# Row-maximum parts moved from VectorE to GpSimd in a two-batch attention and mixture kernel

## The reference

```python
scores = jnp.einsum('bhqd,bhkd->bhqk', Q, K) / jnp.sqrt(jnp.float32(D_HEAD))
scores = jnp.where(causal, scores, jnp.float32(-jnp.inf))
A = jax.nn.softmax(scores, axis=-1)
AV = jnp.einsum('bhqk,bhkd->bhqd', A, V)
```

## Time and profile before

| What | Value |
|---|---|
| Median of 2 runs | 432.5 us (432.46 to 432.53) |
| The profiled execution, its own time | 433.2 us |
| Its span | 431.3 us |
| PE busy | 406.8 us (94%) |
| VectorE busy | 307.0 us (71%) |
| ScalarE busy | 243.2 us (56%) |
| GpSimd busy | 78.4 us (18%), 115 instructions |
| Granted TensorE clock, mean | 0.996 |

### The profile page before, as it was taken

How to read it: one execution, slowest core, us unless ns; L and a number is a source line. 1 busy time by engine, 2 the same in 40 slices (tenths; PEclk the granted TensorE clock), 3 DMA queues, 4 the chain that set the end, 5 groups by cost and what they waited for, 6 DMA issues and landing times.

```text
span 431.3 us, 7424 instructions
## 1 busy us (share of the span) xinstructions
PE 406.8 (94%) x2570; PEld 214.3 (50%) x2570; DVE 307.0 (71%) x807; ACT 243.2 (56%) x541; POOL 78.4 (18%) x115
## 2 busy tenths in 40 slices
PE   7998899999999989999999999999999998999994
PEld 3545444353333544566768844335334344446783
DVE  5538997798799666528478799789879863213765
ACT  5691564766777666543441265667666847642421
POOL 4331210243151010102230021113312011020000
PEclk9999999999999999999999999999999999999998
DMA  6066761450403000001764046054130000000011
GB/s 196 10 101 98 191 105 18 62 88 3 76 2 98 1 2 0 2 1 46 134 124 66 8 91 93 10 86 67 17 60 3 0 3 1 2 0 2 0 50 49
DMA packets 18452, 21.14 MB, mean 49 GB/s; under 512 B 4976, under 2 KB 11888, under 8 KB 18416
## 3 DMA queue, kind: packets, MB, share of 16 engines
q1 hardware_dynamic: 18365, 20.66, 25.7%
q10 hardware_dynamic: 51, 0.01, 0.0%
HBM read 5.79 MB, written 2.10 MB: 18 GB/s over the span
## 4 chain that ended last, share of the span: by engine, by line
PE 74%; DVE 16%; ACT 6%; issue 2%; DMA 1%; POOL 1%; ACTq 0%; DVEq 0%; POOLq 0%
PE ps L951 17%; PE ps L1066 14%; PE ps L1045 14%; PE ps L1022 10%; DVE mx L822 9%; PE ps L959 8%; PE ps L967 4%; PE ps L942 2%; PE ps L1026 2%; ACT pr L681 2%; PE ps L1140 1%; PE ps L1076 1%; DVE ps L818 1%; ACT stk L602 1%; ACT qk_raw L667 1%
## 5 line engine op out<-in xcount | busy, mean ns | idle before, releaser
L681 ACT ACTIVATE pr<-ps 128x512 f32<-128x512 f32 (+3 forms) x384 | 165.9, 495 | 95.2 <-PE ps L1045 93.7
L822 DVE TENSOR_REDUCE mx<-ps 128x1 f32<-128x512 f32 (+3 forms) x240 | 145.6, 666 | 14.5 <-PE ps L1022 7.4
L1045 PE MATMUL ps<-stq,stk 99*128 99x512 bf16 (+3 forms) x384 | 116.2, 330 | 4.4 <-ACT pr L681 3.3
L1022 PE MATMUL ps<-stk,stq 96*128 96x512 bf16 (+3 forms) x384 | 112.7, 327 | 1.9 <-DVE mx L822 0.9
L593 POOL TENSOR_SCALAR_AFFINE_SELECT pr<-pr 128x512 f32<-128x512 f32 x64 | 40.9, 639 | 248.0 <-ACT pr L681 248.0
L1066 PE MATMUL ps<-pr,va 128*32 128x512 f32 (+3 forms) x768 | 81.8, 498 | 0.0
L1045 PEld LDWEIGHTS ps<-stq,stk 99*128 99x128 bf16 x384 | 34.4, 98 | 90.4 <-ACT pr L681 52.0
L1022 PEld LDWEIGHTS ps<-stk,stq 96*128 96x128 bf16 x384 | 37.5, 98 | 22.4 <-issue 6.8
L818 DVE CUSTOM_DVE_ANT_0 ps<-ps,causal 128x384 f32<-128x384 f32 (+1 forms) x64 | 38.6, 648 | 11.6 <-PE ps L1022 11.6
L1026 PE MATMUL ps<-mask,ident_b 128*128 128x128 bf16 x192 | 35.4, 219 | 0.0
L951 PE MATMUL ps<-u_t,avt 128*128 128x256 f32 x128 | 30.8, 384 | 0.3 <-ACT avt L717 0.2
(11 more groups left out here) (108 smaller groups left out, 391.0 us busy)
## 6 DMA issues: line engine op xcount, KB each, us to landing
stq<-qk_raw SPq DMA_DIRECT2D x32, 96.0 KB, 2.8
stk<-qk_raw SPq DMA_DIRECT2D x32, 96.0 KB, 2.8
x_in<-in_x SPq DMA_DIRECT2D x8, 256.0 KB, 3.7
stq<-qk_raw SPq DMA_DIRECT2D x32, 64.0 KB, 2.4
stk<-qk_raw SPq DMA_DIRECT2D x32, 64.0 KB, 2.4
out_y<-x SPq DMA_DIRECT2D x3, 512.0 KB, 3.4
stk<-qk_raw SPq DMA_DIRECT2D x32, 32.0 KB, 2.4
stq<-qk_raw SPq DMA_DIRECT2D x32, 32.0 KB, 2.1
```

Source lines behind the costliest of these rows:

```text
L681: nc.scalar.activation(probs(b, g, s)[:, j, q0 - c * CHUNK:], act_bank(ev)[:, q0 - c * CHUNK:], ACT.Exp, scale=DH ** -0.5).then_inc(s_act_ ...
L822: nc.vector.tensor_reduce(dst, src, AX.X, ALU.max).then_inc(s_dve_free, 1)
L1022: last = nc.tensor.matmul(bank[:, i * w:(i + 1) * w], q[0:ROWS, t // TPC, j, tile(t % TPC)], k[0:ROWS, k0 // CHUNK, j, 0:w], start=True, s ...
L1045: nc.tensor.matmul(bank[:, q0 - c * CHUNK:], stk[stack_of(b, g)][0:ROWS + PARTS, kt // TPC, j, tile(kt % TPC)], stq[stack_of(b, g)][0:ROWS ...
```

## The change

The four instructions of every `split` go to GpSimd. VectorE keeps the reductions and, for the second chunk, the maximum over both halves, which now raises a semaphore of its own, `s_joined`. GpSimd handles `split` at its place in the list and waits for the last maximum (first chunk) or for `s_joined` (second chunk), and for the `rows` matmul that read the parts of the block before it. Each of its four instructions waits for the one before through `s_residue`; the last raises `s_split`, for which PE waits as before.

```diff
+                if kind == "split":
+                    _, _, g, c = ev
+                    whole, n = mx[:, g % 2, c, 0], 3 * (n_split[ev] - 1)
+                    pool.wait_ge(*((s_joined, n_joined[ev]) if c else (s_dve_free, n_last[ev])))
+                    if b * G + g:
+
+                        pool.wait_ge(s_act_full, n_act["rows", *divmod(b * G + g - 1, G), c])
+                    pool.tensor_copy(mhl[:, c, 0], whole).then_inc(s_residue, 1)
+                    pool.wait_ge(s_residue, n + 1)
+                    pool.tensor_tensor(mres[:], whole, mhl[:, c, 0], ALU.subtract).then_inc(s_residue, 1)
+                    pool.wait_ge(s_residue, n + 2)
+                    pool.tensor_copy(mhl[:, c, 1], mres[:]).then_inc(s_residue, 1)
+                    pool.wait_ge(s_residue, n + 3)
+                    pool.tensor_tensor(mhl[:, c, 2], mres[:], mhl[:, c, 1], ALU.subtract).then_inc(s_split, 1)
...
                 if kind == "split":
                     _, _, g, c = ev
 
-                    dve.wait_ge(s_dve_free, last_max)
-                    whole = mx[:, g % 2, c, 0]
                     if c:
-
-                        link(nc.vector.tensor_tensor(whole, mx[:, g % 2, c, 0], mx[:, g % 2, c, 1], ALU.max))
-                    if b * G + g:
-
-                        dve.wait_ge(s_act_full, n_act["rows", *divmod(b * G + g - 1, G), c])
-                    link(nc.vector.tensor_copy(mhl[:, c, 0], whole))
-                    link(nc.vector.tensor_tensor(mres[:], whole, mhl[:, c, 0], ALU.subtract))
-                    link(nc.vector.tensor_copy(mhl[:, c, 1], mres[:]))
-                    nc.vector.tensor_tensor(mhl[:, c, 2], mres[:], mhl[:, c, 1], ALU.subtract).then_inc(s_split, 1)
+                        dve.wait_ge(s_dve_free, n_last[ev])
+                        nc.vector.tensor_tensor(mx[:, g % 2, c, 0], mx[:, g % 2, c, 0], mx[:, g % 2, c, 1], ALU.max).then_inc(s_joined, 1)
```

More of the change, by code:

```diff
@@ L370, in block_kernel @@
         s_split = sem("s_split")
+        s_joined = sem("s_joined")
+        s_residue = sem("s_residue")
         s_rows = [sem(f"s_rows{i}") for i in range(2)]
@@ L406, in block_kernel @@
         n_logits = count("lg")
+        n_last, n_joined = {}, {}
+        for ev in order:
+            if ev[0] == "max":
+                latest = n_dve[ev]
+            if ev[0] == "split":
+                n_last[ev] = latest
+                n_joined[ev] = len([e for e in n_last if e[3]])
         n_split, n_rows = count("split"), count("rows")
@@ L822, in _ @@
                         nc.vector.tensor_reduce(dst, src, AX.X, ALU.max).then_inc(s_dve_free, 1)
-                    last_max = n_dve[ev]
                 if kind == "split":
                     _, _, g, c = ev
-                    dve.wait_ge(s_dve_free, last_max)
-                    whole = mx[:, g % 2, c, 0]
                     if c:
-                        link(nc.vector.tensor_tensor(whole, mx[:, g % 2, c, 0], mx[:, g % 2, c, 1], ALU.max))
-                    if b * G + g:
-                        dve.wait_ge(s_act_full, n_act["rows", *divmod(b * G + g - 1, G), c])
-                    link(nc.vector.tensor_copy(mhl[:, c, 0], whole))
-                    link(nc.vector.tensor_tensor(mres[:], whole, mhl[:, c, 0], ALU.subtract))
-                    link(nc.vector.tensor_copy(mhl[:, c, 1], mres[:]))
-                    nc.vector.tensor_tensor(mhl[:, c, 2], mres[:], mhl[:, c, 1], ALU.subtract).then_inc(s_split, 1)
+                        dve.wait_ge(s_dve_free, n_last[ev])
+                        nc.vector.tensor_tensor(mx[:, g % 2, c, 0], mx[:, g % 2, c, 0], mx[:, g % 2, c, 1], ALU.max).then_inc(s_joined, 1)
                 if kind == "turn":
```

## The result

The changed kernel took 463.9 us (463.63 to 464.15, two runs) against 432.5: a ratio of 1.072, with a 95% interval of 1.070 to 1.074. The forecast was 459, its range 449 to 470. The profiled execution took 463.6 us with a span of 461.8.

A forecast was written before the change was run, and what follows sets the result against it. PE was taken to bound the kernel, holding 74% of the chain. Late masks and parts add 21.8 us and clock falls 4.8, together 26.6 on the 432.5 us median: 459 us predicted, range 449 to 470.

The forecast's parts named there:

- What stands behind the split: On GpSimd, masks PE needs earlier stand behind a split that now waits for VectorE, so they come late.
- The sum of the waits: New PE waits over both batches: 11.6 us in batch 0 and 10.2 in batch 1, together 21.8 us.
- the price of a split on GpSimd: From last maximum to finished parts on GpSimd: four instructions of 0.18 or 0.21 and 0.14 hand-overs, 1.34 us.
- The Trainium skill's factor of two: Two-input elementwise work about twice as slow on GpSimd as VectorE: subtraction 0.34 us, 2.9 us more over eleven places.
- Block (1,1) as the longest: At (1,1) `value` waits for a mask behind the split and two `bo` additions: 4.79 us late in batch 0.
- The clock: PE's clock falls to half in the two longest of four long waits only: 2 x 2.4 = 4.8 us.
- The price per fall: Each clock fall costs 2.4 us, estimated from twenty PE fillers after an idle engine, 7.00 us against 4.58.
- The rival with four falls: Masks late and the clock falls in all four long waits, adding 9.7 us: 464 us, chance 0.22.
- What VectorE gains is hidden: VectorE's busy time falls by some 11 us without use, as it has caught up with PE after such waits.
- Only the latency counts: Rival: VectorE runs close enough behind PE for timely masks; eleven places cost 0.50 us each: 438 us, chance 0.06.

The follow-up runs named there:

- the masks ahead: Changed kernel, with GpSimd taking one or two masks, and the `bo` or `far` between, ahead of the split at five blocks: 434.4 us, ratio 1.0044.
- (1,1) alone: Kernel before, VectorE still splitting, with GpSimd only waiting for the split at block (1,1) in both batches: 443.5 us, ratio 1.026.
- (0,1) alone: Kernel before, VectorE still splitting, with GpSimd only waiting for the split at block (0,1) in both batches: 442.8 us, ratio 1.023.
- seven splits moved: Kernel before, with seven of sixteen splits on GpSimd where PE had not waited, masks ahead at (1,1) and (3,1): 432.6 us, ratio 0.9995.
- `bo` and `far` behind the mask: Changed kernel, with GpSimd's `bo` additions at (1,1) and `far` at (2,1) put behind the first mask: 457.3 us, ratio 1.056.
- fillers inside the waits: Changed kernel plus unused matmuls on PE ahead of long mask waits: 453.4 us; with more ahead of `rows` and one mask too: 451.1 us.

## Why the prediction was right, and where it was off

- *What stands behind the split*: right. The waits for the masks came at (0,1), (1,1) and (2,1), and smaller ones at (1,0), and taking the masks ahead removed nearly everything.
- *The sum of the waits*: 21.8 forecast, 18.2 measured. The term that was mis-sized is the price of a split on GpSimd, 1.34 us. The timeline shows the cast at 64.83 and the last subtraction ending at 65.89, 1.06 us, and VectorE's maximum over both halves had ended 0.07 before: 1.13. The instructions were right, 0.20 and 0.22 against the 0.18 and 0.21 of the lines through the earlier trace rows; the hand-over of 0.14 was not. From one instruction to the next it is 0.08 (65.03 to 65.11). At eleven places 0.21 less makes 2.3 us of the 3.6. Most of the rest lies at the eight places with a mask, where PE's waits came out another 0.1 to 0.2 shorter each.
- *The Trainium skill's factor of two* (GPSIMD Engine Reference, Engine selection) does not hold at this size: 0.22 on GpSimd against 0.17 on VectorE is 1.3.
- *Block (1,1) as the longest*: right, 4.38 us in both batches against 4.79; 0.21 of the difference is again the chain.
- *The clock*: the step that failed is "I let the clock fall in the two longest alone". It fell in or right behind all four long waits, and in a fifth place as well, (2,1) of batch 0, where PE waited 1.08 us for the parts and, one matmul later, 1.57 for the mask. So 4.8 became 12.3. What I read in the earlier trace rows, a fall 2.2 us after the last matmul, spoke for all four; I set it aside because the work ahead of that matmul was thin and ahead of these waits dense. The trace of before does not bear that out: PE was busy for 7.39 of the 7.62 us up to the end of its last matmul, and for 7.65 of the 7.90 up to 62.90, just ahead of the first of the four places. The price per fall met the mean, 2.4 forecast and 2.5 measured, but in part by luck: it came from rows at the opening that show no lower clock, and two falls cost 2.2 us together at (1,1) alone and 5.0 at (0,1) alone.
- *The two errors cancel in part*: 3.6 too many on the waits, 7.5 too few on the clock. That 459 came within 5 us of the 463.9 is to that extent luck. The rival with four falls, 464, met the time by the same cancelling: 21.8 + 9.7 against 18.2 + 12.3.
- *What VectorE gains is hidden*: right; busy time fell by 10.2 us without use, and seven splits moved where nothing else changes gave 0.9995.
- *Only the latency counts*, the rival at 438, is what the run with the masks ahead shows: 434.4, since the chain adds less than I thought.

## What to carry to other kernels

When a step moves to an idle engine that works through a list in order, ask first what stands behind it there, and when that is wanted: the engine's idle time is not free if the step must wait for a slower engine in front of work that was ready. Price the wait, not the instructions: the same sixteen splits, four instructions of 0.2 us each, cost 2 us in the right order and 31 in the wrong one. In this kernel a wait of a few us on TensorE also brought half clock behind it, 12 to 13 us in all, and fillers inside the waits took that part away.

## What was not expected of the hardware

- The clock falls behind shorter waits than thought. It fell in waits of 1.08 and 1.57 us with a matmul between. With `bo` and `far` behind the mask it fell behind 1.11 and 0.35 us, while in the changed kernel's execution the same 1.11 and 0.35 left it alone.
- The stretch at half clock is not set by the wait alone. In the changed kernel it lasted 6.8 us where the wait was 3.0, and at the two waits of 4.4, in one and the same execution, 6.8 in batch 0 and 3.4 in batch 1.
- Half clock costs nearly half of the time that PE works in it: 12.3 of 27.2 us in the changed kernel, 5.1 of 12.2 with the wait at (0,1) alone. The stretch is longer than that, since it can begin while PE still waits, and there it costs nothing more.
- A small GpSimd instruction is nearly as quick as VectorE's: 0.20 and 0.22 us for 128x16 against 0.17, and 0.08 us from one to the next that waits for it.
